# Group norm of an RWKV block: reciprocal root as a power on GpSimd in place of a square root on ScalarE and a reciprocal on VectorE

## What is computed

```python
a4 = att.reshape(b, l, H, S)                  # S = 16, EPS = 1e-5
m = jnp.mean(a4, axis=-1, keepdims=True)
var = jnp.mean((a4 - m) ** 2, axis=-1, keepdims=True)
att = ((a4 - m) * jax.lax.rsqrt(var + EPS)).reshape(b, l, E) * gn_w + gn_b
x = x + att * g @ Wo.T
```

## Time and profile before

| | |
|---|---|
| median of 3 runs | 1711.39 us (1710.81 to 1713.77) |
| the profiled execution: its own time | 1713.96 us |
| its span in the trace | 1712.2 us |
| PE busy | 1594.7 us, 93% of the span |
| DVE busy | 965.3 us, 56% |
| ACT busy | 553.3 us, 32% |
| POOL busy | 644.2 us, 38% |
| granted TensorE clock, mean | 0.97 |
| chain that ended last | PE 75%, DVE 14%, ACT 4%, issue 3%, POOL 2% |

### The profile page before, as it was taken

The page is one execution under the profiler, slowest core; times in us unless marked ns, Lnnn a source line. Parts: engine busy times, 40 slices in busy tenths (PEclk is TensorE's granted clock), DMA queues, the critical chain, the costliest instruction groups (busy, mean ns, idle before and its releaser), DMA issues.

```text
span 1712.2 us, 41121 instructions
## 1 busy us (share of the span) xinstructions
PE 1594.7 (93%) x17600; PEld 1188.1 (69%) x17600; DVE 965.3 (56%) x1942; ACT 553.3 (32%) x898; POOL 644.2 (38%) x540
## 2 busy tenths in 40 slices
PE   4869799999999999999999999999999999999865
PEld 3658577777767677777767777776777777675533
DVE  3263665657666565766566566656656576645312
ACT  1122332334232333434233333433223342333221
POOL 3142432525353352535244253524325252523210
PEclk8889899999999999999999999999999999999888
DMA  7000100101010010101010110101001010100100
GB/s 262 1 26 16 42 13 26 42 16 51 13 55 13 28 39 28 39 15 55 13 38 27 30 40 14 54 13 53 13 26 42 19 48 13 42 13 26 37 25 13
DMA packets 65333, 59.04 MB, mean 34 GB/s; under 512 B 24256, under 2 KB 57408, under 8 KB 64128
## 3 DMA queue, kind: packets, MB, share of 16 engines
q1 hardware_dynamic: 65152, 56.41, 10.6%
HBM read 35.36 MB, written 8.39 MB: 26 GB/s over the span
## 4 chain that ended last, share of the span: by engine, by line
PE 75%; DVE 14%; ACT 4%; issue 3%; POOL 2%; SPq 1%; DMA 1%; POOLq 0%; ACTq 0%; DVEq 0%
PE pair L896 27%; PE pair L904 19%; PE pair L950 5%; PE at_ps L839 4%; PE at_ps L832 3%; PE att_ps L887 3%; PE pair L974 2%; PE pair L930 2%; DVE x L573 2%; PE att_ps L859 2%; DVE kT L486 2%; PE pair L912 2%; PE pair L976 2%; POOL cen L402 2%; PE att_ps L878 1%
## 5 line engine op out<-in xcount | busy, mean ns | idle before, releaser
L896 PE MATMUL pair<-x,wts 128*128 128x256 f32 x2048 | 463.5, 385 | 9.0 <-ACT kT L702 7.6
L896 PEld LDWEIGHTS pair<-x,wts 128*128 128x128 f32 x2048 | 387.9, 192 | 73.2 <-ACT kT L702 12.0
L376 POOL TENSOR_TENSOR x<-x,xnT 128x1024 f32<-128x1024 f32 x80 | 178.5, 2231 | 266.8 <-DVE x L573 266.0
L573 DVE SCALAR_TENSOR_TENSOR x<-pair,vecs,sx 128x256 f32<-128x256 f32 x320 | 132.5, 476 | 191.6 <-PE pair L950 191.6
L713 ACT ACTIVATE at<-at_ps 64x512 f32<-64x512 f32 x256 | 151.1, 590 | 224.1 <-PE at_ps L839 222.3
L904 PE MATMUL pair<-wts,yT 128*128 128x512 f32 x256 | 120.8, 617 | 4.5 <-POOL yT L414 4.5
L896 PE MATMUL pair<-yT,wts 128*128 128x256 f32 x512 | 118.0, 390 | 5.2 <-DVE yT L657 5.2
L904 PE MATMUL pair<-wts,cen 128*128 128x512 f32 x256 | 116.5, 599 | 0.0
L904 PE MATMUL pair<-wts,sx 128*128 128x512 f32 x256 | 114.1, 599 | 1.3 <-ACT cen L697 1.1
L896 PEld LDWEIGHTS pair<-yT,wts 128*128 128x128 f32 x512 | 98.5, 195 | 21.9 <-issue 8.8
L456 DVE SCALAR_TENSOR_TENSOR bonv<-rT,vecs,kT 128x128 f32<-128x128 f32 x128 | 39.0, 367 | 128.2 <-ACT rT L702 78.6
(11 more groups left out here) (134 smaller groups left out, 2602.0 us busy)
## 6 DMA issues: line engine op xcount, KB each, us to landing
rm<-rst SPq DMA_DIRECT2D x1024, 12.0 KB, 1.8
xu<-in_x SPq DMA_DIRECT2D x16, 512.0 KB, 3.8
wts<-in_wts SPq DMA_DIRECT2D x8, 1024.0 KB, 13.4
s<-in_s SPq DMA_DIRECT2D x128, 64.0 KB, 1.8
x<-in_x SPq DMA_DIRECT2D x16, 512.0 KB, 4.4
out<-sx SPq DMA_DIRECT2D x16, 512.0 KB, 3.2
prev<-in_prev SPq DMA_DIRECT2D x32, 4.0 KB, 4.0
maa<-in_maa SPq DMA_DIRECT2D x1, 448.0 KB, 3.8
```

Source lines behind the costliest of these rows:

```text
L376: gp.tensor_tensor(t, t, xnT[:, :, :, 1:L1].rearrange("p g b t -> p (g b) t"), ALU.add).then_inc(x5_ready, 1)
L573: last = ve.scalar_tensor_tensor(seqs(x5[q], g), ps[:, :, g * L:(g + 1) * L], vecs[:, vec, g:g + 1], seqs(sx, g), ALU.add, ALU.mult)
L896: last = pe.matmul(ps[:, g // 2, TB * (g % 2):TB * (g % 2 + 1)], wts[:, m, k, g * P:(g + 1) * P], source[:, k, :], start=(k == 0), stop=(k ...
```

## The change

The square root on ACT (with the table load that stands in front of it) and the reciprocal on DVE go. In their place POOL runs a new piece `gn_pow`, put between `wv` and `mixK` in its order: an addition of eps on 128 x 64 numbers and, after a semaphore, a power of -0.5 on the same 128 x 64 numbers. The division by 16 moves into the square, whose scale becomes 0.25.

```diff
-    "gn_sum": -1, "gn_sub": -1, "gn_square": -1, "gn_var": -1, "gn_std": -1, "gn_rec": -1, "gn_scale": -1,
+    "gn_sum": -1, "gn_sub": -1, "gn_square": -1, "gn_var": -1, "gn_pow": -1, "gn_scale": -1,
...
-ACT_ORDER = ["kt0", "att1", "E0", "gn_square", "z", "gn_std", "E1", "decay", "E2", "k", "yT", "g", "vtm1",
+ACT_ORDER = ["kt0", "att1", "E0", "gn_square", "z", "E1", "decay", "E2", "k", "yT", "g", "vtm1",
...
-DVE_ORDER = ["mixW", "attb1", "chain1", "gn_sum", "kv0", "wv", "gn_var", "mixK", "c02_1", "gn_rec", "mixG",
+DVE_ORDER = ["mixW", "attb1", "chain1", "gn_sum", "kv0", "wv", "gn_var", "mixK", "c02_1", "mixG",
...
-POOL_ORDER = ["mixW", "gn_sub", "rch1", "wv", "mixK", "gn_scale", "mixG", "c02_1", "rch1b", "ln1_stats",
+POOL_ORDER = ["mixW", "gn_sub", "rch1", "wv", "gn_pow", "mixK", "gn_scale", "mixG", "c02_1", "rch1b", "ln1_stats",
...
+                elif name == "gn_pow":
+                    gp.wait_ge(gvar_ready, c.count(1, 1))
+                    gp.tensor_tensor(gvar[:, :], gvar[:, :], epsc[:, 0:1].broadcast_to([P, NB * G * HG]), ALU.add)\
+                      .then_inc(gstd_ready, 1)
+                    gp.wait_ge(gstd_ready, c.count(1, 1))
+                    gp.tensor_tensor(grs[:, :], gvar[:, :], half[:, 0:1].broadcast_to([P, NB * G * HG]), ALU.pow)\
+                      .then_inc(grs_ready, 1)
...
-                elif name == "gn_rec":
-                    ve.wait_ge(gstd_ready, c.count(1, 1))
-                    ve.reciprocal(grs[:, :], grs[:, :]).then_inc(grs_ready, 1)
...
-                    ac.activation(sq, kk, ACT.Square).then_inc(sq_ready, 1)
-                elif name == "gn_std":
-                    ac.wait_ge(gvar_ready, c.count(1, 1))
-                    ac.activation(grs[:, :], gvar[:, :], ACT.Sqrt, bias=epsc[:, 0:1], scale=1.0 / S)\
-                      .then_inc(gstd_ready, 1)
+                    ac.activation(sq, kk, ACT.Square, scale=0.25).then_inc(sq_ready, 1)
```

## The result

The changed kernel takes 1861.11 us in the median of 4 runs (1859.45 to 1863.19), against 1711.10 us for the kernel before in the same comparison (1708.58 to 1713.77). The ratio is 1.088, with a 95% interval of 1.086 to 1.090: slower by 150 us. The profiled execution takes 1859.45 us, 145.5 more than that of before.

A forecast was written before the change was run, and what follows sets the result against it. PE was taken as nearly always busy, paced through DVE and ACT by POOL's train; 15 x 3.2 = 48 us plus 2.5 in the last group norm gave + 50.5, so 1762 us for the median, range 1727 to 1995.

The forecast's parts named there:

- What bounds the kernel now: The end of POOL's train sets DVE's chain1b, then ACT, then PE, whose projection g waits 7.6 us in all.
- What is removed: ACT's table load and square root and DVE's reciprocal lie beside other work, worth 0; 1.07 us once in last group norm.
- What is added: On POOL ahead of mixK: addition 0.30 us, semaphore 0.08, power 3.2 (ends 0.81 and 16.6).
- rival 2: Power on POOL paid per column, 8 us or more: 1976 us, 2005 with clock loss, 1930 if DVE unheld; chance 0.24.
- the forecast's own case: A power on POOL between 1.3 and 8 us, kernel at 1735 to 1865 us; chance 0.47.
- The mechanism of the sum: Longer POOL train ends chain1b on DVE 3.2 us later, delaying PE's projection g in 15 steps: 48 us.
- D: The time by which POOL's train gets longer per step, forecast at 3.5 us (ends 1.15 and 16.9).
- What would show the forecast right: In the new profile: chain1b's fifth and sixth instruction stretched, g's wait about 3 us, period 101.6 us.
- The hold on DVE: One DVE instruction of chain1b slips in per POOL instruction, so chain1b gets going only when POOL's train ends.
- The clock: PE's granted clock falls behind long waits: at most 29 us more, counted only for a power paid per column.
- The tail: Last group norm: 0.30 + 0.08 + 3.2 in place of 1.07 us, so + 2.5 us.

## Why the prediction was right or wrong

**What bounds the kernel now: right.** That the end of POOL's train sets DVE, ACT and PE is shown by c02_1 moved back (-6.5 us, against -6 expected) and by the power of 16 columns (DVE stretched at each POOL instruction, PE's g waiting 3.07 us).

**What is removed: right.** The table load, the square root and the reciprocal were put at nothing, and their removal, with the addition of eps put in, measures 1.0008. The square (128 x 1024) takes 1.06 us with the scale in it as without.

**What is added: the step that failed.** It is the price of the power in the sum: "I take the geometric middle of the power's own part, 0.51 x 5.7 = 2.9 us, so 3.2 us for the instruction": it takes 10.53. Of the 0.70 us at 2 columns only 0.39 are fixed and 0.157 are paid per column. So it was rival 2, paid per column, at 62% of its upper bound of 0.254 per column. Between ends 20 times apart the geometric middle was a choice without a row behind it. The price was to be multiplied by 64, so even a modest share per column dominates. The measured 1861 us do lie in the stretch given to the forecast's own case (1735 to 1865), but that is luck: the own case had a power of at most 8 us.

**The mechanism of the sum: right at the size forecast, wrong at the real one.** With D = 3.2 the wait is at projection g through DVE. With the real D = 0.29 + 0.08 + 10.53 - 0.04 = 10.86 it is at projection k through mixK. The prediction had that slack (2.9 us) and, in rival 2, the formula for a power that does not hold DVE: 10.86 - 2.9 - 0.5 = 7.5 us per period. PE's idle time did grow by 7.5. What would show the forecast right (the fifth and sixth instruction of chain1b stretched, g waiting 3 us for ACT's k) is absent in the changed kernel.

**The hold on DVE: there beside POOL's ordinary instructions, absent beside the power.** Rival 2's 15 x 16.6 takes the power to hold DVE for its whole length. No row of before showed that, and the runs show the contrary. With the power of 16 columns L491 took 2.13 us beside mixK's addition. Beside the full power it took 0.28, as the same instruction does with POOL quiet, and the copy L496 0.36. The recorded sum with D = 3.5 does not rest on a hold by the power: the one of 2.91 us was over at 824.59, before DVE came to chain1b at 824.74. Why the power leaves DVE free is open: an addition of that length on few columns was not tried. Why most of its price is paid per column is not shown by any run either.

**The clock: named, but only as an addition to the extreme case.** It costs 28 us in the changed kernel, and 1.4 to 2.1 us per period in the mean already behind waits of 3 us, where the forecast's own case counted none. So the recorded sum had a second term too small: with a power of 2.9 us the kernel takes 1777.66 us, and 1762 were forecast for one of 3.2.

**The rest.** The tail: the last group norm was to cost the new instructions less 1.07 us. By the same formula 0.3 + 0.1 + 10.5 - 1.07 = 9.8, and from the last `gn_sub` to the end of the span there are 10.1 us more (77.2 against 67.1). Full steps with a projection k behind a power: the forecast counted 15, the traces have 14. Two of the 15 waits in the earlier trace rows lie at 50.01 and 133.74 us, ahead of the first `gn_sub` (198.11).

## What to carry to other kernels

A price read at one size says little of another size when fixed and per-element parts are unknown. If nothing in the trace separates them, the size ratio belongs in the forecast. Here the price lay at 62% of the upper end, where the geometric middle had put it at 18%. POOL's order worked as a queue here (mixK's addition starts at 859.84, where the power ends), so what is inserted ahead of a piece with 2.9 us of slack costs all that it exceeds this slack (7.5 us per period for D = 10.86), and one place further back is worth 78 us here. A wait on TensorE costs more than its length if the clock falls behind it (some 28 of the 150 us here), and GpSimd's ordinary instructions stretch VectorE's (L491 2.13 us in place of 0.28), so moving two of them off a critical VectorE chain was worth more than removing work from two engines that were waiting anyway (6.5 us against nothing).

## What the runs showed of the hardware

- A power on GpSimd (tensor_tensor, fp32) takes 0.39 us plus 0.157 to 0.160 us per column of 128 partitions: 0.70, 2.91, 5.42 and 10.53 us at 2, 16, 32 and 64 columns. An addition on 64 columns takes 0.30.
- A power on 32 or 64 columns does not hold up VectorE instructions that GpSimd's additions and multiplications on 256 to 1024 columns hold up (L491 took 0.28 us beside the powers of 32 and 64 columns, 2.13 us beside mixK's addition on 1024; the fourth instruction of chain1b, on 128 x 32, took 0.86 us beside c02_1's addition on 256 in the kernel before, 0.22 beside the power of 64).
- Behind a wait of PE of 2.9 to 3.3 us the next 32 matmuls mostly took 8.6 to 8.9 us in place of 7.17 (7.14 to 10.21 in all), behind one of 7.96 us 8.53 to 9.98. With the wait filled with matmuls they took 7.17.
